# Attention of the first layer: scores computed a second time transposed, row maxima as rows of the contraction, values in float32 on 32 columns a head

## The reference, cut to what matters

```python
Q = split_heads(Xn @ Wq + bq)
K = split_heads(Xn @ Wk + bk)
V = split_heads(Xn @ Wv + bv)
scores = jnp.einsum('bhqd,bhkd->bhqk', Q, K) / jnp.sqrt(jnp.float32(D_HEAD))
causal = jnp.tril(jnp.ones((n_ctx, n_ctx), dtype=bool))
scores = jnp.where(causal, scores, jnp.float32(-jnp.inf))
A = jax.nn.softmax(scores, axis=-1)
AV = jnp.einsum('bhqk,bhkd->bhqd', A, V)
AV = AV.swapaxes(-2, -3).reshape(X.shape[:-1] + (D_MODEL,))
return AV @ Wo + bo
```

## Time and profile before

| | us |
|---|---|
| median of 3 runs | 1127.68 (1126.4 to 1129.34) |
| the profiled execution: its span | 1155.7 |
| PE busy in it | 957.4 (83%) |
| DVE busy | 746.7 (65%) |
| ACT busy | 657.2 (57%) |
| POOL busy | 458.8 (40%) |

### The profile page before, as it was taken

One profiled execution on the slowest core, in us unless ns is written; L12 is line 12 of the kernel. 1 busy time (PEld: TensorE's weight loads), 2 busy tenths in 40 slices (PEclk: granted clock), 3 DMA queues, 4 the chain that ended last, 5 costly groups with the idle time before them and its releaser, 6 DMA issues. The chain is left out here.

```text
span 1155.7 us, 21305 instructions
## 1 busy us (share of the span) xinstructions
PE 957.4 (83%) x5505; PEld 801.8 (69%) x5505; DVE 746.7 (65%) x1932; ACT 657.2 (57%) x1705; POOL 458.8 (40%) x641
## 2 busy tenths in 40 slices
PE   6678799999978744687999994078989998999994
PEld 2466688888866633465899994056867777888883
DVE  4885799999974753338755552799746777444453
ACT  3568889999972333327766663367853334433331
POOL 3477556666640566501344443457620111200000
PEclk8788999999997766798999997589989998999997
DMA  7067844444404422307543434730032232102012
GB/s 250 13 210 178 216 108 91 91 91 92 91 8 138 154 75 91 133 14 253 188 129 121 130 121 151 257 116 1 12 104 70 87 108 76 47 28 65 28 56 87
DMA packets 109867, 123.53 MB, mean 107 GB/s; under 512 B 44192, under 2 KB 82848, under 8 KB 109656
## 3 DMA queue, kind: packets, MB, share of 16 engines
q1 hardware_dynamic: 101128, 99.19, 30.5%
q0 software_dynamic: 8656, 23.33, 5.5%
HBM read 77.87 MB, written 44.62 MB: 106 GB/s over the span
## 5 line engine op out<-in xcount | busy, mean ns | idle before, releaser
L746 ACT ACTIVATE PR<-PS,nmax 128x128 f32<-128x128 f32 (+3 forms) x256 | 135.6, 551 | 12.6 <-DVE nmax L786 11.2
L663 POOL TENSOR_SCALAR PR<-PR,rinv 128x128 f32<-128x128 f32 (+3 forms) x256 | 132.3, 536 | 0.0
L786 DVE TENSOR_REDUCE nmax<-PS 128x1 f32<-128x128 f32 (+3 forms) x256 | 113.7, 481 | 20.2 <-PE PS L689 14.8
L1384 POOL DMA_INDIRECT r_results<-r_y,r_to x79 | 76.0, 963 | 112.8 <-DVE r_to L1439 76.6
L794 DVE TENSOR_TENSOR PTlo<-PS,PThi 128x512 fp32r<-128x512 f32 (+1 forms) x192 | 103.1, 590 | 2.9 <-ACT PThi L756 2.9
L756 ACT ACTIVATE PThi<-PS 128x512 fp32r<-128x512 f32 (+1 forms) x192 | 96.7, 545 | 6.1 <-PE PS L701 6.0
L688 PE MATMUL PS<-K,Q 128*128 128x128 f32 (+3 forms) x256 | 83.4, 385 | 12.0 <-DMA Q<-q_parts 8.9
L701 PE MATMUL PS<-ident,PR 128*128 128x128 f32 x640 | 85.8, 279 | 3.2 <-DVE PTlo L794 2.6
L717 PE MATMUL PS<-PThi,V 128*128 128x512 f32 (+3 forms) x256 | 85.1, 345 | 1.0 <-DVE PTlo L794 0.5
L2511 DVE TENSOR_TENSOR H<-PS,H 128x256 f32<-128x256 f32 x72 | 30.6, 424 | 81.9 <-ACT H L2472 80.2
L2472 ACT ACTIVATE H<-PS 128x256 f32<-128x256 f32 x72 | 27.6, 385 | 97.2 <-PE PS L2631 96.1
(11 more groups left out here) (393 smaller groups left out, 3099.5 us busy)
## 6 DMA issues: line engine op xcount, KB each, us to landing
r_xg<-r_sorted SPq DMA_DIRECT2D x79, 129.0 KB
r_wst<-in_routed SPq DMA_DIRECT2D x16, 608.0 KB
K<-k_parts SPq DMA_DIRECT2D x64, 128.0 KB
Q<-q_parts SPq DMA_DIRECT2D x32, 128.0 KB
Q<-q_parts SPq DMA_DIRECT2D x64, 64.0 KB
V<-v_parts SPq DMA_DIRECT2D x64, 64.0 KB, 2.4
mlp_st<-r_results SPq DMA_DIRECT2D x8, 512.0 KB, 7.2
c_yg<-r_results SPq DMA_DIRECT2D x8, 512.0 KB, 8.3
```

Of the source, the lines that this page charges most:

```text
L663: pool.tensor_scalar(PR[:, e % 4, i, 0:w], PR[:, e % 4, i, 0:w], rinv[:, e % 4, i:i + 1], 1.0, ALU.mult, ALU.mult).then_inc(norm_done, 1)
L746: act.activation(PR[:, e % 4, i, 0:w], k.PS[:, i, 0:w], ACT.Exp, bias=nmax[:, e % 4, i:i + 1], accum_out=rsum[:, e % 4, i:i + 1]).then_inc ...
L786: dve.tensor_reduce(nmax[:, e % 4, i:i + 1], k.PS[:, i, 0:P * (i + 1)], AX_X, ALU.max, negate=True).then_inc(max_done, 1)
L1384: pool.indirect_dma_start(out=d.results, out_offset=bass.IndirectOffsetOnAxis(ap=to[:, i % TO_LANES:i % TO_LANES + 1], axis=0), in_=y[:, i ...
```

## The change

- Queries and keys are loaded three quads deep, two heads side by side: one head's 48 rows (query high, high, low against key high, low, high) at partition 0, the other's at 64. Rows 48 and 49 of the keys are ones.
- A step handles a pair of heads; there are 32, in straight-line code. The scores of the pair are made as before, without further use than the maxima: VectorE reduces both heads' tile in one instruction. The negated maximum is split into two float32r halves, transposed to four rows (shift_rows), copied to mrow by ScalarE and moved by two DMAs of SyncE into rows 48 and 49 of each head's queries.
- Two steps later TensorE makes the scores again, transposed (columns): keys as weights, 50 rows, so that the maximum is already subtracted; the mask is added transposed. ScalarE's exponential writes float32 probabilities, keys on the partitions. Transposes of probabilities, high and low halves and the normalisation on GpSimd are gone.
- Values: float32 products with a head's 32 columns (16 of values, 16 ones, which give the row sums) as weights, into 32 partitions of bank 6 a head. VectorE writes V in that layout straight out of PSUM in the input stage; the detour of the values through memory is gone.
- A quad's result is copied (osb), transposed back (rows), divided by its sums (normalize), and a batch's results are transposed once more into OT, in two blocks of 128 rows instead of four quads of padded rows. So the output weights need one DMA and half the splitting, and products makes half as many products.

```diff
...
+            sp.wait_ge(heads.filled, KQ_LANES)
             heads.wait_stored(sp, 0)
-            for u in range(2):
-                heads.load_keys(sp, 0, u, u)
-                heads.load_values(sp, 0, u, u)
+            for quad in range(2):
+                heads.load(sp, quad)
             store(2)
-            sp.wait_ge(heads.s_ready, 16)
-            heads.load_keys(sp, 0, 2, 0)
+            heads.load(sp, 2)
             store(3)
...
+                    for t in range(2):
+                        last = dve.tensor_tensor(heads.V[:, b, 2 * g + t, :, 0:DH], k.PS[:, 6 + g, t * D:(t + 1) * D].rearrange("p (h d) -> p h d", d=DH),
+                                                 bv[:].rearrange("p (h d) -> p h d", d=DH), ALU.add)
+                    last.then_inc(vf_done, 1)
...
+KQ_LANES = 3
+ROWS = 3 * DH
+SHIFT = ROWS + 2
+PAIRS = B * QUADS * 2
+S_ORDER = (3, 0, 2, 1)
+CHUNK_AT = (0, 4 * P, 7 * P, 9 * P)
+UNITS = ((0, 4 * P), (4 * P, 3 * P), (7 * P, 3 * P))
...
+        self.V = k.sb("V", [P, B, TT, HEADS, 2 * DH], F32, c, "right")
+        self.Q = [k.sb(f"Q_{u}", [P, 2, T], F32R, c, "right") for u in range(KQ_LANES)]
+        self.K = [k.sb(f"K_{u}", [P, 2, T], F32R, c, "right") for u in range(KQ_LANES)]
...
+    def fill(self, pool):
+        for u in range(KQ_LANES):
+            pool.memset(f32(self.K[u][:]), 1.0).then_inc(self.filled, 1)
+        pool.memset(self.V[:].rearrange("p b t h e -> p (b t h) e")[:, :, DH:2 * DH], 1.0).then_inc(self.filled, 1)
+    def load(self, sp, n, halves=range(2)):
+        b, q, u = n // QUADS, n % QUADS, n % KQ_LANES
         for j in halves:
             r, heads = 64 * j, slice(j, 4, 2)
...
+            keys, queries = self.k.k_parts[b, q, heads], self.k.q_parts[b, q, heads]
+            sp.dma_start(f32(self.K[u][r:r + 32]), keys.rearrange("s a r t -> (a r) s t")).then_inc(self.kq_in[u], 16)
+            sp.dma_start(f32(self.K[u][r + 32:r + 48]), keys[:, 0].rearrange("s r t -> r s t")).then_inc(self.kq_in[u], 16)
+            sp.dma_start(f32(self.Q[u][r:r + 16]), queries[:, 0].rearrange("s r t -> r s t")).then_inc(self.kq_in[u], 16)
+            sp.dma_start(f32(self.Q[u][r + 16:r + 48]), queries.rearrange("s a r t -> (a r) s t")).then_inc(self.kq_in[u], 16)
...
+        PT = k.sb("PT", [P, 2, 2, 10 * P], F32, c)
+        A = k.sb("A", [P, 2, TT, D], F32, c)
+        osb = k.sb("osb", [P, T], F32, c)
+        mrow = k.sb("mrow", [4, 2, T], F32, c)
...
+            def load(n, half):
+                if half == 0 and n % QUADS == 0:
+                    heads.wait_stored(sp, n // QUADS)
+                sp.wait_ge(st_ready, 6 * (n - KQ_LANES + 1))
+                heads.load(sp, n, (half,))
+            for x in range(PAIRS):
+                sp.wait_ge(m_copied, x + 1)
+                for j in range(2):
+                    row = 64 * j + ROWS
+                    sp.dma_start(f32(Q[x // 2 % KQ_LANES][row:row + 2, x % 2, :]), mrow[2 * j:2 * j + 2, x % 2, :]).then_inc(m_in[x % 2], 16)
+                n = (x + 3) // 2 if x % 2 else (x + 2) // 2
+                if x >= 3 and n < PAIRS // 2:
+                    load(n, 1 - x % 2)
...
+            def scores(u):
+                def stage(x):
+                    lane, p, i, unit = x // 2 % KQ_LANES, x % 2, S_ORDER[u], 4 * x + u
+                    if u == 0 and p == 0:
+                        pe.wait_ge(kq_in[lane], 128 * (x // 2 // KQ_LANES + 1))
+                    w = P * (i + 1)
+                    if unit >= 2:
+                        pe.wait_ge(max_done, unit - 1)
+                    for j in range(2):
+                        r = slice(64 * j, 64 * j + ROWS)
+                        pe.matmul(S_BANK(u, j)[:, 0:w], Q[lane][r, p, P * i:P * i + P], K[lane][r, p, 0:w], start=True, stop=False)
+                    for j in range(2):
+                        last = pe.matmul(S_BANK(u, j)[:, w - P:w], k.identb[:], k.maskb[:], start=False, stop=True)
+                    last.then_inc(s_ready, 1)
+                return stage
+            def columns(u):
+                def stage(x):
+                    lane, p = x // 2 % KQ_LANES, x % 2
+                    if u == 0:
+                        pe.wait_ge(m_in[x % 2], 32 * (x // 2 + 1))
+                    wait(pe, exp_done, 3 * x + u)
+                    for n in ((0,), (1,), (2, 3))[u]:
+                        at, w = CHUNK_AT[n] - UNITS[u][0], T - P * n
+                        for j in range(2):
+                            r = slice(64 * j, 64 * j + SHIFT)
+                            pe.matmul(ST_BANK(j)[:, at:at + w], K[lane][r, p, P * n:P * n + P], Q[lane][r, p, P * n:T], start=True, stop=False)
+                        for j in range(2):
+                            last = pe.matmul(ST_BANK(j)[:, at:at + P], k.maskb[:], k.identb[:], start=False, stop=True)
+                    last.then_inc(st_ready, 1)
+                return stage
+            def wait_side(kind, i):
+                if turns:
+                    before, n = turns[-1]
+                    pe.wait_ge({"shift": m_copied, "rows": a_done, "columns": aT_lo}[before], n + 1)
+                turns.append((kind, i))
+            def shift_rows(x):
+                pe.wait_ge(shift_done, x + 1)
+                wait_side("shift", x)
+                for t in range(TT):
+                    last = pe.transpose(side(t)[0:4, :], f32(shift[:, x % 2, t].rearrange("p j a -> p (j a)")), k.ident[:])
+                last.then_inc(mT_ready, 1)
+            def values(half):
+                def stage(x):
+                    q, p = x // 2, x % 2
+                    if half == 0:
+                        if x == 0:
+                            pe.wait_ge(heads.filled, KQ_LANES + 1)
+                        pe.wait_ge(exp_done, 3 * x + 3)
+                        wait(pe, o_copied, q)
+                    for n in ((0, 3), (1, 2))[half]:
+                        w = T - P * n
+                        for j in range(2):
+                            s = 2 * p + j
+                            last = pe.matmul(O[32 * s:32 * s + 32, P * n:T], V[:, q // QUADS, n, 4 * (q % QUADS) + s, :],
+                                             PT[:, x % 2, j, CHUNK_AT[n]:CHUNK_AT[n] + w], start=(n == 0), stop=(n == 2))
+                    if half:
+                        last.then_inc(av_done, 1)
+                return stage
+            def rows(q):
+                pe.wait_ge(o_copied, q + 1)
+                wait_side("rows", q)
+                for t in range(TT):
+                    last = pe.transpose(side(t), osb[:, t * P:(t + 1) * P], k.ident[:])
+                last.then_inc(oT_ready, 1)
...
             inputs.tensor(pe)
-            loop(pe, body)
+            wavefront((0, scores(0)), (0, scores(1)), (2, columns(0)), (1, shift_rows), (3, values(0)), (4, quads(rows)), (5, batches(attended(0))),
+                      (0, scores(2)), (2, columns(1)), (0, scores(3)), (2, columns(2)), (3, values(1)), (5, batches(attended(1))), n=PAIRS)
...
+            def attended_row(q):
+                act.wait_ge(av_done, 2 * (q + 1))
+                wait(act, oT_ready, q)
+                act.activation(osb[:], O, ACT.Copy).then_inc(o_copied, 1)
+            def exponential(u):
+                def stage(x):
+                    at, w = UNITS[u]
+                    act.wait_ge(st_ready, 3 * x + u + 1)
+                    if u == 0:
+                        wait(act, av_done, x - 1)
+                    act.activation(PT[:, x % 2, :, at:at + w], k.PS[:, 4:6, 0:w], ACT.Exp).then_inc(exp_done, 1)
+                return stage
+            def shift_row(x):
+                act.wait_ge(mT_ready, x + 1)
+                if x >= 2:
+                    act.wait_ge(m_in[x % 2], 32 * (x // 2))
+                act.activation(mrow[:, x % 2, :], SIDE[0:4, :], ACT.Copy).then_inc(m_copied, 1)
...
             inputs.scalar(act)
-            loop(act, body)
+            wavefront((4, quads(attended_row)), (2, exponential(0)), (1, shift_row), (5, batches(high(0))), (2, exponential(1)), (2, exponential(2)),
+                      (5, batches(high(1))), n=PAIRS)
...
+            def maximum(u):
+                def stage(x):
+                    i = S_ORDER[u]
+                    dve.wait_ge(s_ready, 4 * x + u + 1)
+                    dve.tensor_reduce(nmax[:, x % 2, i, :], k.PS[:, 2 * (u % 2):2 * (u % 2) + 2, 0:P * (i + 1)], AX_X, ALU.max,
+                                      negate=True).then_inc(max_done, 1)
+                return stage
+            def split_shift(x):
+                dve.wait_ge(max_done, 4 * (x + 1))
+                wait(dve, mT_ready, x - 1)
+                own.link(dve.tensor_copy(shift[:, x % 2, :, :, 0], nmax[:, x % 2]))
+                own.wait()
+                dve.tensor_tensor(shift[:, x % 2, :, :, 1], nmax[:, x % 2], f32(shift[:, x % 2, :, :, 0]), ALU.subtract).then_inc(shift_done, 1)
+            def normalize(q):
+                dve.wait_ge(oT_ready, q + 1)
```

(53 more changed lines are left out.)

275 lines of the change are left out of this document (44 added, 231 removed).

## The result

The changed kernel takes 1181.1 us (median; 1175.3 to 1189.7) against 1128.5 for the kernel before in the same comparison: 1.048 times as long, 95% interval 1.043 to 1.053. The forecast was 1165 us, with 1108 to 1222 as its range and slower as its likeliest sign. The profiled execution of the changed kernel spans 1180.8 us. One of the four executions of experiment 10's kernel took 2445.9 us, and without it the median of that kernel is 1231.8 us and not 1234.0.

The account below looks back on a forecast made before the run. Three engines were full and TensorE was to decide, its step growing from 7.15 to 8.2 us. Attention ending 42.3 us later, less 4 behind it, made +38.3, scaled to +37.4: 1165 us, range 1108 to 1222.

Parts of the forecast that it names:

- What decides: Attention: relief of VectorE, ScalarE and GpSimd counts only if TensorE's step gets shorter; it was forecast at 8.2 against 7.15 us.
- signs of being wrong: Attention: step under 7 us, first transposed scores near 100 us, or ScalarE or the loads ending TensorE's waits.
- wait for the second exponential: TensorE's step: the third part of the transposed scores waits for banks still read by that exponential, 0.5 us.
- nothing for the other 17: TensorE's step: of some 19 changes of product shape only the two out of the float32 values cost, 0.4 us.
- rival (c): TensorE's step: every change of shape waits, 16 more at 0.09 us; step 9.4, 1200 us; chance 0.20.
- the side-by-side end: TensorE's scores of two heads: both row halves run fully together, 1.3 us; the forecast took the middle, 1.75.
- in order of issue only the second record of one head and the first of the other can meet: TensorE's values: two heads' float32 products overlap only in part, 2.9 us between 4.3 in turn and 2.15 side by side.
- rival (a): TensorE's step: the array overlaps what it can, shape changes free, values near 2.5; step 6.45, 1114 us; chance 0.20.
- The start: Attention's start: first transposed scores wait for rows of maxima behind SyncE's loads and stores, until 120 us.
- The end: Attention's end: thirty full steps, 246 us, then a drain of 20; end at 386 us, 42.3 later than before.
- Behind it: Output stage: fewer products save 3.0 us and halved weight splitting 1, together -4.
- Scaling the difference by the ratio of the two times of before: Total: profiled execution exceeds the median run by a factor of 1.025, so +38.3 us became +37.4.

Follow-up runs that it names:

- experiment 10: Changed kernel with all values of the pair's first head in the first place and all of the second's in the second, other work between; 1234.0 us, 1.096 times before.
- experiment 4: Changed kernel with each head's mask product cut into two 64-row products in the row tiles of the scores; 1148.5 us, 1.020 times before.
- experiment 9: Changed kernel with the second head's values issued after the first's within each half, not in pairs; 1180.7 us, no difference.
- experiment 1: The kernel before, unchanged, profiled a second time; it spans 1124.3 us, against 1155.7 in the first profile.
- experiment 2: Changed kernel with the copies of the maxima into the queries started by GpSimd's queue, not SyncE's; 1162.8 us, 1.036 times before.
- experiment 3: Changed kernel with the second half of each load of queries and keys started with the first, one step sooner; 1181.5 us, no gain.
- experiment 7: Changed kernel with only the third unit of scores moved behind the second part of the transposed scores; 1164.6 us, 1.037 times before.

## Why the prediction was right or wrong, point by point

**What decides: right.** ScalarE and VectorE fell under 50% and gave nothing, since TensorE's step grew. TensorE became the only bound, and the sign followed. ScalarE and the loads did end waits of TensorE, one of the signs of being wrong, but with 12.1 and 4.2 us over thirty steps, near the 0.5 and 0.1 a step that the sum gave them.

**The step: a sum close to the clean one, by errors that cancel.**

| term, us a step | forecast | measured |
|---|---|---|
| scores and scores transposed | 1.75 + 1.75 | 2.24 + 2.16 |
| maxima as rows | 0.44 | 0.53 |
| values, with the changes of shape behind them | 2.9 + 0.4 | 2.40 |
| results back to rows | 0.33 | 0.48 |
| wait for the second exponential | 0.5 | 0.44 |
| late loads, lowered clock | 0.1 | 0.33 |
| sum | 8.2 | 8.58 |

The measured column is the step above; 0.48 is half of the 0.66 us by which every second undisturbed step is longer and an eighth of the further 1.18 of every eighth; 0.33 is the rest to the mean step of 8.58 from 193.5 to 373.6 us. Three terms were wrong, in opposite directions; that the sum came near the clean step is luck.

The step that failed on the loss side is "nothing for the other 17" changes of shape, decided by the earlier trace rows. Experiment 4 shows that a change between the 64-row scores and the 128-row masks costs: two changes a unit, 0.2 us together, so about 0.1 apiece, near rival (c)'s 0.09. The fence of a step shows it in place: masks followed by the transposes of maxima, which have 128 rows too, take 0.12 us (298.42 to 298.54), masks followed by 64-row scores 0.22 (300.64 to 300.86). That is also the rule of the Trainium skill that the forecast weighed (TensorEngine Tiling (Array Packing), Key Properties); here the trace agrees with it. Line 1298, which looked free, changed only the columns; so did line 494, and neither row bore on a change of rows.

The scores themselves were taken too dear, at the middle of two ends. Side by side they do run: the 0.38 us of a 384-column unit in experiment 4 is for both heads and four half masks. Without the changes of shape between scores and masks the eight units take 2.98 us there, where the forecast has 1.75 + 1.75 and the side-by-side end 2.6. This hid some 0.5 of the 1.4 us that the changes cost.

The step that failed on the gain side is "in order of issue only the second record of one head and the first of the other can meet". They overlap almost entirely, rival (a)'s value (2.5 there, 2.40 with the changes of shape behind it). Experiment 9 shows that order of issue was the wrong thing to reason from, experiment 10 what the overlap is worth.

**The start: right mechanism, 4.5 us early.** SyncE's order did hold the first transposed scores, from 101.9 to 115.5 and not 120. Two terms were off against each other: issues are cheaper (a quad's load 5.1 us, from 95.15 to 100.20, where 6.4 was taken; the last batch's stores 6.5, from 100.20 to 106.73, where 9.1 was; the copy issued at 107.85 and not near 117), and the landing dearer (115.5, so 6.4 us after the second issue at 109.1, where 2.3 was taken).

**What was not foreseen: the lower clock.** The granted clock was 0.52 from 94 to 140 us, and it fell before the stall. The forecast counted all thirty steps at full clock. The first eight from 115.5 took 78.4 us, 9.8 each and 12.8 more than forecast, the largest part of the miss. The stall is not shown to be its cause: in experiment 2, without the long stall, these steps took 67.1 us, but behind stalls of 11.8 and 13.2 us, in experiments 3 and 9, they took 71.0 and 69.6. Those two kernels lost the time later; all three take 265 to 266 us for the thirty steps. What sets these stretches stays open.

**The end.** Thirty steps took 265.8 us and not 246 (12.8 of the difference in the first eight, 7.0 in the other 22). Undisturbed, at 7.77 + 0.48, they would have taken 247.5, so nearly all of it is lowered clock and late loads. The drain took 22.1 us and not 20, with waits of 0.9 us for exponentials that nothing covers any more. With the start 4.5 earlier: 17.5 us later than forecast.

**Behind it.** The output stage gave 2.4 us, not 4. Scaling the difference by the ratio of the two times of before had no ground: experiment 1 shows that the extra 30 us of that execution lay in one stage. It took 0.9 us off, which hardly matters here; with a larger difference it would have.

**The total.** On the profiles: the forecast's 38.3, and 17.5 at attention's end, and 1.6 in the output stage, less 1.1 by which attention ends later in the second profile of before, make 56.3; the spans differ by 56.5. The medians differ by 52.6, where 37.4 was forecast.

## What to carry to other kernels

Count the changes of TensorE's shape: products of 64 rows with one of 128 rows between them pay about 0.1 us at each change, and splitting the small product into the tiles of its neighbours won 33 us here. Narrow products in different column tiles are worth putting next to each other: 2.1 us a step here, and within a group of four it made no difference which head's came first. A copy in the middle of a dependency loop belongs on a queue with nothing ahead of it: that saved 9 to 10 us of stall here. And a gain that exceeds the wait it removed wants a second pair of kernels before it is credited to the edit.

## What the runs showed of the hardware that was not expected

- By the trace, TensorE starts products of different column tiles out of the order in which the program issues them: in experiment 9 two products that are issued four records apart began 14 ns apart.
- Two float32 products on 32 columns each overlap almost fully: 2.27 us for one head, 1.20 for a half of two heads with as many columns in all.
- After the stall of 13.6 us the granted clock was 0.50 from 116 to 140 us, with TensorE busy 23.9 of these 24; behind the stall of experiment 3 it was full 12.6 us after work began again. And kernels with the same products had a granted clock of 0.91 (experiment 3) to 1.00 (experiment 7) from 200 to 330 us, with TensorE busy 96 and 95% of it. What makes the lowered stretches within attention was not found.
